# TensorE's order at the end of a step: the z product ahead of the transposition of u

## The reference

```python
def block(h, p):                                  # one of four layers
    k, q, v = split(h @ wkqv)
    r = tril(q @ k.T / sqrt(d)) / (1 + sqrt(position))
    r = r / clip(abs(r.sum(-1)), 1)
    a, gate = split((r @ v) @ w1 + b1)
    m = (a * silu(gate)) @ w2 + b2
    m = groupnorm1(m, gg, gb)                     # over tokens and features of a batch
    y = m + h
    f = gelu(y @ wf1 + bf1) @ wf2 + bf2
    return layernorm(f + y, lg, lb)
# the other branch, for each token: its best of 8 experts
g = silu(expert_weight * (gelu(xn @ w1[e] + b1[e]) @ w2[e] + b2[e]))
```

## Time and profile before

| | |
|---|---|
| median of 3 runs | 507.23 us (507.22 to 507.36) |
| profiled execution | 506.84 us, its span 504.9 us |
| mean granted PE clock | 0.986 |
| PE busy | 469.9 us, 93% of the span |
| DVE busy | 383.9 us, 76% |
| ACT busy | 253.4 us, 50% |
| POOL busy | 259.6 us, 51% |

### The profile page before, as it was taken

The page is one execution under the profiler, slowest core; times in us unless marked ns, Lnnn a source line. Parts: engine busy times, 40 slices in busy tenths (PEclk is TensorE's granted clock), DMA queues, the critical chain, the costliest instruction groups (busy, mean ns, idle before and its releaser), DMA issues.

```text
span 504.9 us, 9876 instructions
## 1 busy us (share of the span) xinstructions
PE 469.9 (93%) x3157; PEld 392.3 (78%) x3157; DVE 383.9 (76%) x1342; ACT 253.4 (50%) x533; POOL 259.6 (51%) x285
## 2 busy tenths in 40 slices
PE   6999889999999999999999999999999999999751
PEld 4887666766889888988888898889888988767431
DVE  4768887788867767777787677777767777889986
ACT  3823334444566554565655446656554565455320
POOL 4520188888454455544545554544455556445542
PEclk9999999999999999999999999999999999999896
DMA  9998411111611111110111111111111000510022
GB/s 264 236 127 204 174 38 39 34 37 58 130 60 43 58 44 59 59 65 31 49 49 51 53 63 59 59 38 38 59 43 59 33 12 6 152 27 1 26 79 62
DMA packets 47345, 35.05 MB, mean 69 GB/s; under 512 B 13320, under 2 KB 38736, under 8 KB 47296
## 3 DMA queue, kind: packets, MB, share of 16 engines
q1 hardware_dynamic: 44496, 28.94, 22.1%
q0 software_dynamic: 2272, 4.71, 2.8%
q10 hardware_dynamic: 528, 0.79, 0.5%
HBM read 14.70 MB, written 9.42 MB: 48 GB/s over the span
## 4 chain that ended last, share of the span: by engine, by line
PE 65%; POOL 12%; DVE 11%; issue 6%; DMA 2%; ACT 1%; POOLq 0%; SPq 0%; DVEq 0%; ACTq 0%
PE bank L1272 8%; PE bank L1199 7%; PE bank L1183 7%; POOL x_slots L471 6%; PE pair L1346 4%; PE pair L1318 4%; PE bank L1210 4%; PE pair L1300 4%; PE bank L1359 4%; PE bank L1211 4%; PE bank L1212 4%; PE pair L1348 3%; PE pair L1298 3%; POOL ln_rs L426 2%; PE bank L1254 2%
## 5 line engine op out<-in xcount | busy, mean ns | idle before, releaser
L483 POOL TENSOR_TENSOR zhat<-zhat,all_lg 128x512 f32<-128x512 f32 x31 | 42.5, 1373 | 88.1 <-PE bank L1244 74.1
L1272 PE MATMUL bank<-all_f,G_sb 128*128 128x128 f32 x512 | 74.2, 278 | 0.0
L656 ACT ACTIVATE y_sb<-bank,gn_bi,gn_sc 128x512 f32<-128x512 f32 x32 | 24.9, 778 | 97.3 <-DVE gn_bi L1050 97.3
L1272 PEld LDWEIGHTS bank<-all_f,G_sb 128*128 128x128 f32 x512 | 68.6, 195 | 1.4 <-issue 1.4
L651 ACT ACTIVATE uT_h<-bank 128x512 fp32r<-128x512 f32 x32 | 19.1, 597 | 97.5 <-PE bank L1254 97.5
L426 POOL TENSOR_TENSOR ln_rs<-ln_ve,half_neg 128x4 f32<-128x4 f32 x32 | 33.4, 1045 | 34.7 <-DVE ln_ve L680 34.4
L1183 PEld LDWEIGHTS bank<-moe_w,h_T 128*128 128x128 f32 x312 | 39.5, 191 | 13.8 <-issue 13.8
L568 ACT ACTIVATE h_T<-bank,w_t 128x128 f32<-128x128 f32 x156 | 44.5, 372 | 5.1 <-PE bank L1199 5.1
L523 POOL DMA_INDIRECT y_rows<-yt,slot_info x39 | 40.9, 1049 | 11.0 <-POOL yt L520 11.0
L636 ACT ACTIVATE G_sb<-bank,all_par 128x512 f32<-128x512 f32 x64 | 43.0, 694 | 7.1 <-PE bank L1235 4.7
L503 POOL TENSOR_TENSOR gn_rs<-gn_ve,half_neg 128x1 f32<-128x1 f32 x32 | 18.5, 578 | 51.4 <-DVE gn_ve L898 51.3
(11 more groups left out here) (178 smaller groups left out, 1241.3 us busy)
## 6 DMA issues: line engine op xcount, KB each, us to landing
w_t<-moe_w SPq DMA_DIRECT2D x39, 258.0 KB, 2.4
x_slots<-moe_w SPq DMA_DIRECT2D x1, 2515.5 KB, 21.6
xt<-x_slots SPq DMA_DIRECT2D x39, 64.0 KB, 1.8
x_sb<-in_L_attn_x SPq DMA_DIRECT2D x8, 256.0 KB, 5.7
moe_w<-in_L_ffn_w SPq DMA_DIRECT2D x1, 2048.0 KB, 19.0
moe_w<-y_rows SPq DMA_DIRECT2D x8, 256.0 KB, 4.6
out<-moe_w SPq DMA_DIRECT2D x7, 256.0 KB, 2.3
all_f<-in_L_attn_Wf SPq DMA_DIRECT2D x2, 512.0 KB, 4.3
```

The source lines that it names most:

```text
L483: pool.tensor_tensor(zhat[:, b % 2, :, :], zhat[:, b % 2, :, :], all_lg[:, li, :].unsqueeze(1).broadcast_to([P, C, D]), ALU.mult)\
L1272: last = mm(bank[7][:, at_c], G_sb[:, k, at_c], all_f2[:, li, k, :], start=False, stop=k == 1)
```

## The change

In the steps that have u's transposition and z, other than steps 2 to 6, PE now takes z first, then u's transposition, then the means. No instruction is added or taken away, and the lists of ACT, DVE, POOL and SP stay as they are. Steps 0 and 1 have no z, and the three drain steps have no u, so that the instructions change places in 25 steps: 7 to 31.

```diff
                 for stage in ((gelu_second, means, u_by_feature) if first and 2 <= t < B - 1 else
-                              (means, gelu_second) if l == L else (u_by_feature, gelu_second, means)):
+                              (means, gelu_second) if l == L else (gelu_second, u_by_feature, means)):
                     stage(l, t)
```

## The result

| | before | after |
|---|---|---|
| median | 507.23 us (507.11 to 507.36, 4 runs) | 533.62 us (533.46 to 533.79, 4 runs) |
| ratio, 95% interval | | 1.0521 (1.0509 to 1.0533) |
| span of the profiled execution | 504.9 us | 531.8 us |
| mean granted PE clock | 0.986 | 0.983 |

A forecast was written before the change was run, and what follows sets the result against it. PE bounds the kernel (busy 93%), level with a relay through DVE and ACT. Terms 20.0 + 2.0 + 1.1 + 0.7 + 1.3 + 1.6 = 26.7 us on 506.84 make 533.5, plus 0.39: 533.9 us, range 528 to 538.

The forecast's parts named there:

- The relay: Chain from PE's u transposition through DVE and ACT to tile_back; u 2.22 us later, less 1.02 waiting, leaves 1.11.
- No slack in front of `tile_back`: Entering 18 parted steps, PE already held by h_T at L1183, so 1.11 us each (0.94 to 1.21), 20.0 in all.
- rival 2: Only part of the delay reaches PE: 0.6 us per parted step, 17.5 in all, 524.7 us; chance 8%.
- Steps 8, 15 and 22: Entries without an EARLY tile: scores wait for q_sb, 0.66 us each (bounds 0.56 and 1.11), 2.0 in all.
- Steps 30, 31 and 32: Entries into these steps: L893 later by 0.71, 1.31 and 1.59 us.
- PE's wait for `u_sb`: Ends of steps 29 to 31: z fills this wait; 0.35 us gained into step 30, and the wait is gone.
- z earlier is worth nothing: z comes 0.44 us earlier, but its reader L671 stands behind uT_l and L893 on DVE: gain 0.
- Rival 1: The shift is swallowed by slack over 1.11 us in L893's chain; only gains left, 506.1 us; chance 4%.
- Rival 3: Later DVE chain meets POOL's long operations elsewhere, sum 4 us or so higher, 538 us; chance 12%.
- Rival 4: PE idles about 2.2 us where step 32 begins; clock falls to 1.2 GHz, 1.4 to 3 us, 536; chance 8%.
- PE's busy time: Whole kernel: PE's busy time in microseconds stays about as it is.
- PE's share: Whole kernel: PE's busy share of the span, 93% before, falls to some 88%.

The follow-up runs named there:

- two blocks of z and three: Kernel before, with two or three of z's four column blocks ahead of u's transposition in steps 7 to 31: 507.57 us and 519.86 us.
- dve_means_first: The changed kernel, but DVE takes gn_moments before split_u in steps 2 to 31: 519.11 us, ratio 1.0233.
- h_T_yt_first: The changed kernel, with ACT's h_T ahead of y_sb and DVE's EARLY tile_out (L1081) ahead of the sums of S: 550.57 us, ratio 1.0856.

## Why the prediction was right, point by point

**The relay and its slack.** The step that carried everything was to set the 2.22 us of u's delay against DVE's 1.02 us of waiting for the means, and to take only the rest. Measured: 1.12 in L893, and the corner between two blocks of z and three, with no slack left at two. That DVE's order turns u's lateness into lateness of the group norm was inferred from the code, and `dve_means_first` shows it.

**No slack in front of `tile_back`.** I read this from register operations 0.06 us behind `h_T`, and took the full 1.11 between bounds of 0.94 and 1.21. Measured 1.10. It is made of two terms that I had used only for the bounds, and that nearly cancel: L1183 starts 0.15 behind `h_T`, where it was 0.21, so that 0.06 was slack, and its eight matmuls take 1.15 us in place of 1.09, since the first load is uncovered. The register operations of the changed kernel stand at the same place, right behind `h_T`, which ends at 286.02:

```profile
L1183 PEldq FUSED_REGOPS  x4: 46/48/51, 286.1 to 286.4; - x4
```

What the prediction did not say is that a second and third arm (L1081 to L1199, L1096 to L1210) stand just behind the first. It made the forecast safer than I could claim: rival 2 needed all arms to have slack.

**Steps 8, 15 and 22**: mis-sized, 0.66 against 0.53. At the start of step 15 of the changed kernel:

```profile
238.70 0.78 ACT L656 ACTIVATE y_sb<-bank,gn_bi,gn_sc 128x512 f32<-128x512 f32 x1 [2.45 <-DVE gn_bi L1050]
239.38 0.59 ACT L610 ACTIVATE q_sb<-pair 128x512 f32<-128x512 f32 x1
...
240.01 1.16 PE L1318 MATMUL pair<-q_sb,hT 128*128 128x128 f32 x8 [0.25 <-ACT q_sb L610]
```

`q_sb` follows `y_sb` after 0.68 us. In the kernel before it started at 231.38, 0.82 after `y_sb`, since it also had to wait for PE's L1300 (until 231.34). I had shifted `q_sb` by the whole 1.11, but 0.14 of it was slack against PE. The uncovered first load was as priced: L1318 takes 1.16 in place of 1.05. 0.56 less 0.14, and 0.10 for the load, make 0.52.

**Steps 30, 31 and 32**: each 0.1 short (0.81, 1.40 and 1.68 for 0.71, 1.31 and 1.59). I gave z a start 0.86 behind L1359, from a place where L1359 had not waited. In these steps L1359 has waited and its first load is uncovered, so that z starts 0.96 behind it, as the end of step 30 shows:

```profile
476.15 1.13 PE L1359 MATMUL bank<-gg_sb,all_w 128*128 128x512 f32 x2 [0.23 <-DVE gg_sb L939]
...
477.11 0.27 PE L1270 MATMUL bank<-ident,y_sb 128*128 128x128 f32 x1
```

The same 0.10 that I had used two items earlier was missing here. The gain in it, PE's wait for `u_sb`, was there: L1254 no longer waits.

**The sum** is closer than its terms. The parted steps were 0.2 us too high together, steps 8, 15 and 22 0.4 too high, steps 30 to 32 0.3 too low, and the drain's 0.5 was not in it. That these offset one another to 0.2 is luck; that 18 steps of 1.1 carry the result is not.

**z earlier is worth nothing**: right. L671 stands behind L893, and got later with it.

**The rivals.** Rival 1 (slack) and rival 2 (part) did not come. Rival 3 did not come in the change: L929 and L914 take in each step what they took before. But `h_T_yt_first` shows that its mechanism is real here, at 1.09 us a step (16.86 for 15.77).

Rival 4, the clock, came where I had put it, and its price did not. In step 32 PE idles for 2.65 us in front of L1210, where it was 0.66, and from 497.0 on the granted clock is 0.50, which is 1.2 GHz; four of the six 512-column matmuls then take 0.43 us each to the next start, in place of 0.23. The kernel before had its own slow stretch later in the same step, and there the changed kernel is at full clock:

```profile
497.50:500.50 3.00, 3.00 (x10) 2.33 (x8) 2.39 (x12) 1.97 (x4) 1.01 (x1) 0.54 0.17 48
500.50:505.00 4.50, 3.65 (x10) 1.44 (x8) 4.46 (x5) 1.71 (x4) 3.57 (x3) 1.00 0.01 4
```

What I had left out is that PE waits behind these matmuls: for 2.19 us in front of L1359 in the kernel before, for 0.56 now. The slow stretch fits into that wait. L1359 starts at 501.87 for 475.55, 26.32 later, and L893 of step 31, before the slow stretch, had been as late to 0.01.

In the drain the clock falls once more. PE does nothing for 2 us, and then takes the means and z at a granted 0.51, nearly all at 1.2 GHz:

```profile
505.00:507.00 2.00, 0.00 (x0) 0.00 (x0) 1.90 (x4) 0.44 (x1) 2.00 (x2) 1.00 0.44 131
507.00:510.50 3.50, 3.43 (x16) 3.43 (x17) 2.22 (x9) 0.62 (x1) 0.95 (x2) 0.51 0.00 0
```

The same z had 1.00 in the kernel before, and took 1.4 us less. This stretch does show in the time: L893 of step 32 is 26.51 later, by the slower means, and the statistics of z behind it 26.61. So 0.3 of the drain's 0.5 us stand behind the slow stretch. The other 0.25 arise after it, where long operations of DVE (L842, L865) and POOL (L483, L487) meet in another order than before.

The clock is not what raised PE's busy time to 476.2 us, where I had said that it would stay. Of the 6.3 us more, 4.9 stand in steps 7 to 27, 0.21 to 0.24 in most of them, with the clock at 1.00, and only 1.7 behind the start of step 31's scores. At the entry to a parted step L1183's longer first load is 0.06 of it; the rest I take to be the end of the last matmul before the wait, which the next one used to overlap, but no run separates it. PE's share fell to 90%, not to 88%. The 18 waits of 0.88 us left the granted clock at 1.00.

## What to carry to other kernels

When an engine's work is put in another order, follow the one that gets later through every list that it passes, and stop at the first idle time: up to that idle time the delay is free. Beyond it the delay is paid in every round of the loop in which the busiest engine has no slack against that list: here nearly in full in 18 steps, and by half in the three that have no EARLY tile. A kernel in which the busiest engine never waits may have several feeders level with it; register or issue operations that start right behind a semaphore's release, and not early, show it before any wait does. Where a feeder's operation is moved ahead and the time does not fall, the next arm was level too, and the operations must be looked at for their durations as well as their order: one that starts a few hundredths behind another engine's, and not ahead of it, can take more than twice as long.

## What the runs showed of the hardware that was not expected

A DVE operation with two SBUF inputs (L929) took 1.77 us beside a POOL operation on SBUF (L483) that had started 0.06 us earlier, and 0.68 us alone. Holding POOL back until it was done was worth 19 us of 550. It was not slowed in proportion to the overlap: in the eleven traces there are 73 cases in which L929 or L914 starts while POOL's L483 or L487 runs, and in every one it ends 0.54 to 0.56 us after POOL's operation has, whether it had started 0.05 or 1.17 us behind it. The kernel before has five such cases, in steps 27 to 31 (1.17 us twice, 1.37 us three times). Where DVE's operation started first, by 0.03 to 0.04 us, it took its 0.68 us and POOL's took 1.78 to 1.80 for 1.27. DVE's L939, which takes one of its inputs from PSUM, was not held: it started at 298.48, in the middle of POOL's L487 (from 297.88, 1.61 us), and took 0.73 us, as everywhere else.

The Trainium skill (SBUF — State Buffer, SBUF: two separate sides) says that VectorE and GpSimd share a port pair by an exclusive lock, which an operation of VectorE with two SBUF inputs takes part in against one of GpSimd that reads SBUF: whoever starts first has it for the whole instruction. By that rule L929 would be blocked until 297.80 and then run its own 0.68; the trace has it end at 298.34, 0.54 after, so all but 0.14 us agrees. The case the other way round is 0.13 us short in the same way.
